# Moving the second layer norm's last step two slots earlier in a fused cross-attention layer, and writing its reciprocal root with one more VectorE instruction

## The reference

```python
q = (query @ Wq + bq); k = (key @ Wk + bk); v = (values @ Wv + bv)      # split into 16 heads
scores = einsum('bhqd,bhkd->bhqk', q, k) / sqrt(32)
scores = where(j < i, scores, -1e30); attn = softmax(scores)            # row 0 is set to 0
attn_out = einsum('bhqk,bhkd->bhqd', attn, v) @ Wo + bo
x = layer_norm(query + attn_out, ln1_g, ln1_b)
ffn = relu(x @ W1 + b1) @ W2 + b2
out = layer_norm(x + ffn, ln2_g, ln2_b)
# layer_norm(x) = (x - mean) * rsqrt(var + 1e-5) * g + b
```

## Time and profile before

| | |
|---|---|
| median of three runs | 2712.73 us |
| profiled execution, its own time | 2712.73 us |
| span from the first to the last instruction | 2710.8 us |
| TensorE busy (matmul) | 2620.6 us, 97% |
| VectorE busy | 2098.2 us, 77% |
| GpSimd busy | 1582.1 us, 58% |
| ScalarE busy | 1529.8 us, 56% |
| mean granted TensorE clock | 0.986 |

### The profile page before, as it was taken

One profiled execution on the slowest core, in us unless ns is written; L12 is line 12 of the kernel. 1 busy time (PEld: TensorE's weight loads), 2 busy tenths in 40 slices (PEclk: granted clock), 3 DMA queues, 4 the chain that ended last, 5 costly groups with the idle time before them and its releaser, 6 DMA issues.

```text
span 2710.8 us, 61812 instructions
## 1 busy us (share of the span) xinstructions
PE 2620.6 (97%) x22604; PEld 2241.0 (83%) x22604; DVE 2098.2 (77%) x4723; ACT 1529.8 (56%) x2945; POOL 1582.1 (58%) x1724
## 2 busy tenths in 40 slices
PE   7999999999999999977999999999999999999998
PEld 5888888888888888765888888888888888888887
DVE  6888888888888888877767766777767676767675
ACT  4777777777777777766434343444343444444443
POOL 3777777766666666655545454555545555555553
PEclk9999999999999999987999999999999999999999
DMA  6556555655555555555322231323232323132220
GB/s 191 149 147 157 144 147 146 159 148 142 149 135 134 138 138 133 141 134 142 98 53 69 50 70 49 70 49 72 54 69 50 71 49 70 49 69 52 67 54 26
DMA packets 439552, 273.31 MB, mean 101 GB/s; under 512 B 299648, under 2 KB 334400, under 8 KB 439248
## 3 DMA queue, kind: packets, MB, share of 16 engines
q1 hardware_dynamic: 438288, 267.79, 39.6%
q10 hardware_dynamic: 960, 1.57, 0.3%
HBM read 109.86 MB, written 57.67 MB: 62 GB/s over the span
## 4 chain that ended last, share of the span: by engine, by line
PE 83%; DVE 10%; issue 3%; DMA 1%; SPq 1%; POOL 1%; ACT 1%; ACTq 0%; DVEq 0%; POOLq 0%
PE h_ps L1359 24%; PE acc L1375 21%; PE lin_ps L707 10%; PE front L1345 6%; PE lin_ps L703 5%; PE max_ps L682 5%; PE st_ps L729 4%; PE o_ps L749 3%; PE o_ps L751 2%; DVE max_ps L660 2%; PE st_ps L764 2%; DVE xT L509 2%; DVE V L628 1%; DVE negmax_parts L603 1%; DVE W L1266 1%
## 5 line engine op out<-in xcount | busy, mean ns | idle before, releaser
L422 POOL TENSOR_TENSOR prob_lo<-probs,prob_hi 128x512 f16<-128x512 f32 (+1 forms) x768 | 788.1, 1041 | 408.7 <-ACT prob_hi L501 406.9
L1359 PE MATMUL h_ps<-x_halves,W 128*128 128x256 f16 x6144 | 756.5, 273 | 5.7 <-ACT hf L1173 5.7
L1359 PEld LDWEIGHTS h_ps<-x_halves,W 128*128 128x128 f16 x6144 | 596.5, 98 | 92.0 <-issue 15.9
L1375 PE MATMUL acc<-W,hs 128*128 128x256 f16 x5376 | 669.5, 273 | 1.1 <-DVE hs L1319 1.0
L1173 ACT ACTIVATE hf<-h_ps,b1s,scale_evac 128x256 f32<-128x256 f32 x512 | 284.4, 561 | 548.4 <-PE h_ps L1359 546.3
L1375 PEld LDWEIGHTS acc<-W,hs 128*128 128x128 f16 x5376 | 525.9, 98 | 62.4 <-issue 1.6
L499 ACT ACTIVATE probs<-st_ps 128x512 f32<-128x512 f32 (+1 forms) x768 | 406.9, 530 | 287.5 <-PE st_ps L764 248.6
L660 DVE CUSTOM_DVE_ANT_0 max_ps<-max_ps,mask_q 128x256 f32<-128x256 f32 (+2 forms) x768 | 421.7, 563 | 136.6 <-PE max_ps L682 136.3
L1099 POOL TENSOR_TENSOR hf<-hf 128x256 f32<-128x256 f32 x256 | 241.0, 941 | 471.4 <-ACT hf L1173 470.9
L501 ACT ACTIVATE prob_hi<-st_ps 128x512 f16<-128x512 f32 (+1 forms) x768 | 407.9, 531 | 0.0
L1319 DVE TENSOR_TENSOR hs<-hf,hs 128x896 f16<-128x896 f32 x256 | 285.8, 1136 | 154.1 <-ACT hs L1162 154.1
(11 more groups left out here) (120 smaller groups left out, 3845.3 us busy)
## 6 DMA issues: line engine op xcount, KB each, us to landing
heads<-stage SPq DMA_DIRECT2D x756, 128.0 KB, 2.4
raw<-in_xT SPq DMA_DIRECT2D x64, 256.0 KB, 3.1
o_in<-ctx_rows SPq DMA_DIRECT2D x256, 64.0 KB, 2.7
x_in<-in_x SPq DMA_DIRECT2D x32, 512.0 KB, 4.1
x_rows<-x SPq DMA_DIRECT2D x64, 256.0 KB, 2.0
o_in<-x_rows SPq DMA_DIRECT2D x256, 64.0 KB, 2.4
out<-y SPq DMA_DIRECT2D x32, 512.0 KB, 3.1
raw<-in_cT SPq DMA_DIRECT2D x60, 256.0 KB, 3.6
```

Source lines behind the costliest of these rows:

```text
L422: pool.tensor_tensor(prob_lo[:, k % 4, 0:w], probs[:, k % PROBS, 0:w], prob_hi[:, k % 4, 0:w], ALU.subtract).then_inc(pl_done, 1)
L1359: last = pe.matmul(h_ps[:, f % 2, 0:T], W1[:, aw, j, f * P:(f + 1) * P], x1_halves[:, item.parity, aa, j, :], start=(j == 0 and m == 0), s ...
L1375: last = pe.matmul(acc_products[:, n, :], hs[:, p % HS, aa, n, :], W2[:, p, aw, n, :], start=(p == 0 and m == 0 and n % 2 == 0), stop=(p = ...
```

## The change

`NORM2`, the slot of the second layer norm's root on ScalarE and of its `normalise` on VectorE, goes from `RES2 + 8` to `RES2 + 6`, that is from slot 14 of a window to slot 12; `STORE` goes from `RES2 + 9` to `RES2 + 8`, slot 15 to slot 14. In `normalise`, which both layer norms use, the Newton step z = r(1.5 - 0.5 r r ve) is written with four instructions behind the reciprocal in place of three.

```diff
-    NORM2 = RES2 + 8
-    STORE = RES2 + 9
+    NORM2 = RES2 + 6
+    STORE = RES2 + 8
...
-    LNS = 2 * U + 4
+    LNS = 2 * U + 5
...
             dve.reciprocal(r, sd[:, norm, :]).then_inc(ln_step[norm], 1)
             wait_for(dve, ln_step[norm], LNS, item, 2 * U + 2)
-            dve.scalar_tensor_tensor(out=t, in0=r, scalar=-0.5, in1=r, op0=ALU.mult, op1=ALU.mult
-                                     ).then_inc(ln_step[norm], 1)
+            dve.tensor_tensor(t, r, r, ALU.mult).then_inc(ln_step[norm], 1)
             wait_for(dve, ln_step[norm], LNS, item, 2 * U + 3)
             dve.tensor_tensor(t, t, ve[:, norm, :], ALU.mult).then_inc(ln_step[norm], 1)
             wait_for(dve, ln_step[norm], LNS, item, 2 * U + 4)
-            dve.scalar_tensor_tensor(out=z, in0=t, scalar=1.5, in1=r, op0=ALU.add, op1=ALU.mult
-                                     ).then_inc(ln_root[norm], 1)
+            dve.tensor_scalar(t, t, -0.5, 1.5, ALU.mult, ALU.add).then_inc(ln_step[norm], 1)
+            wait_for(dve, ln_step[norm], LNS, item, 2 * U + 5)
+            dve.tensor_tensor(z, r, t, ALU.mult).then_inc(ln_root[norm], 1)
```

## The result

The changed kernel takes 2759.2 us, the median of four runs (2754.3 to 2761.5), against 2712.2 for the kernel before (2711.5 to 2712.9). The ratio is 1.0171, with a 95% interval from 1.0153 to 1.0188: 1.7% slower, 47.0 us (41 to 51 by the interval), where 2760.3 us were forecast. The profiled execution took 2753.78 us, with a span of 2751.9.

The account below looks back on a forecast made before the run. TensorE, busy 1350.00 of 1350.00 us in the second stage, was taken as the bound. 30 windows x 1.57 = 47.1, plus 0.2 and 0.3, gave 47.6 us on 2712.73: 2760.3 us, range 2722 to 2778.

Parts of the forecast that it names:

- What bounds the kernel, and through what: Second stage: TensorE always busy, so the change can only lose; margin of 2.84 us at tile 15, through evacuation 13.
- The turns with GpSimd: Second norm's chain on VectorE: instructions wait for GpSimd's running ones, including b2 additions; TensorE loses 1.57 us per window.
- the working: One window's chain after the change: reciprocal 2014.57, transpose 2020.94, evacuation 13 to 2023.72, tile 15 at 2023.77 (was 2022.20).
- The tensor_scalar: New one-input VectorE step in `normalise`: waits in turn too, or else the sum is 0.2 us per window lower; left open.
- Thirty windows, and it does not wear off: Full windows: root and GpSimd's sums both hang on evacuation 11, so the stall returns; 30 x 1.57 = 47.1 us.
- A second stall: Next window's tile 0: just fits with 0.3 us to spare; as a rival, another 1 us per window, 2790 us, chance 0.07.
- The signs named: Profile after: TensorE short about 1.6 us per window; last small step 1.2, first large step 1.7, high half waits 5.
- The rival without a meeting with the additions: Second norm's chain misses the b2 additions; evacuation 13 is 0.27 us ahead of tile 15; 2713.2 us, chance 0.11.
- The other edits: Fourth small step outside the second norm's chain, hidden behind TensorE's full queue in 29 windows: 0.2 + 0.3 us.
- the 0.2 priced: Very end of the kernel, nothing beside the chain: the fourth small step adds 0.19 us.
- The 0.3 us put down for the first windows: First layer norm in the first three windows, where TensorE has gaps: the fourth small step costs perhaps 0.3 us in all.
- The store: Earlier `STORE`: block reads queued behind it need both transposes done, so no cost, no gain.

Follow-up runs that it names:

- slot 13: The changed kernel with NORM2 in slot 13 in place of 12 (`RES2 + 7`), STORE in slot 14: 2720.2 us, ratio 1.0033.
- slot 11: The changed kernel with NORM2 one slot earlier still (`RES2 + 5`), ScalarE's root behind evacuation 10 instead of 11: 2711.7 us, ratio 1.0000.

## Why the prediction was right

*What bounds the kernel, and through what.* Right: TensorE's queue was full, so the change could only lose, and it lost at tile 15 through evacuation 13, which stands on ScalarE behind a wait for VectorE's transpose.

*The turns with GpSimd.* Right in each step checked. From the start of evacuation 11, the working had the reciprocal 0.68 us on, the large steps at 3.74 and the transpose at 7.05; measured are 1985.70, 1988.75 and 1992.06 less 1985.01, that is 0.69, 3.74 and 7.05. Tile 15 stood at 9.88 in the working and stands at 9.85. That the two engines take turns was read from a handful of rows and now shows in 30 windows. The experiment with the additions of b2 two slots later shows that this, and not the amount of work ahead of the transpose, makes the loss.

*The tensor_scalar.* Left open between waiting and not; it waits. Asked for at 1987.11, it ends at 1987.50 with GpSimd's line 1102 (1987.47), where it takes 0.17 with GpSimd idle (2010.58 above). The trace of the kernel before could have settled it, with the `tensor_scalar` of `variance`, which takes 0.17 undisturbed (at 2003.35) and here ends with GpSimd's sum:

```profile
2010.30 0.73 POOL L1100 TENSOR_TENSOR hf<-hf 128x256 f32<-128x256 f32 x1
2010.57 0.48 DVE L1190 TENSOR_SCALAR ve<-mv 128x2 f32<-128x2 f32 x1
```

The reciprocal, with one input as well, does not wait: it takes 0.15 to 0.17 in all 64 places of either trace, also right behind the start of a sum (1985.70). The rule of the Trainium skill cited there ("SBUF — State Buffer", "SBUF: two separate sides") agrees.

*Thirty windows, and it does not wear off.* Right: 30 waits of 1.18 or 1.19, and 30 x 1.55 = 46.5 us. The experiment with the root behind evacuation 10 shows why: root and GpSimd's sums hang on the same evacuation. That the totals agree to 0.6 us (47.6 and 47.0) is luck all the same, as the interval reaches from 41 to 51. The two profiled executions differ by 41.1: 7.7 less ahead of the first evacuation of line 1173, 3.6 more in the first two windows (1.55 of it the first stall), 45.0 more in the 29 that follow, and 0.2 at the end.

*A second stall.* Right that it just fits. It was put at 0.3 us ahead of tile 0; the second low half ends at 1996.84 and tile 0 starts at 1997.16. With the chain in slot 13 this is the place where 0.2 us per window is lost.

*The signs named.* The last small step (1.18 for 1.2), the first large step (1.72 in 30 windows, for 1.7) and the high half's wait (4.92 for 5) came as said. TensorE's busy time does not fall short by 1.6 us per window but by 1.18; the rest of the 1.55 shows only in the distance of starts.

*The rival without a meeting with the additions.* It was priced too tight. The run with the additions later is that case, and its large steps start 2.72 us behind evacuation 11 (2014.91 to 2017.63), where the rival's sum has 2.92: it gives the fourth step 0.4 and not the 0.2 that it adds undisturbed. So 0.51 us are left ahead of tile 15, and not 0.27.

*The other edits.* Here the sum was right and the reason was not. At the very end, the chain takes 0.99 us from the reciprocal to the large steps (2746.25 to 2747.24), against 0.78 before (2705.43 to 2706.21), the 0.2 priced. Outside the second norm's chain, the fourth instruction was priced at 0.2 to 0.5 us in all, because TensorE's queue covers it. Put alone into the kernel before, in both norms, it costs 13 us. In the change the first norm's is covered all the same: the `hs` of slot 8 ends 1.87 us ahead of need in every full window, where it was 0.4 to 2.1. The likely reason is that the second norm's chain no longer stands ahead of the `hs` of slot 14 and the store is out of the way early; no run takes the two apart. So the sum held, but the reason given for this term ("hidden behind TensorE's full queue") says nothing of the margin, and by it I expected 2712.4 to 2713.0 us of the Newton step alone, which took 2724.3. The 0.3 us put down for the first windows is not borne out either: they took 2.0 us more than the stall, in this one pair of profiles, and the spread ahead of 1340 us is larger than that.

*The store.* No cost, as worked out: the block reads behind it start at 1995.14, as soon as the second transpose is over, though the store itself went out at 1991.16.

Two things stay open. Why VectorE's lateness differs from window to window before the change was not settled; in the later windows the reads ahead of the projection also take longer on the queue (5.8 to 6.9 us instead of 5.5 from the first block read to `x_in`), which fits, but no run took them apart, and in the change such reads (5.9 to 6.2) in the last windows leave the distance of 46.4 as it is. And the runs of one kernel spread by some 7 to 12 us, of which the profiles put a good part ahead of 1340 us: there the profiled execution of the change is 7.7 us ahead of that of before (first evacuation of line 1173 at 1247.69 and 1255.43), without any edit in that stretch that would make it faster.

## What to carry to other kernels

When an instruction moves, ask which instruction of another engine is started by the same event; two engines released together meet in every round, and a move of one slot may end it (slot 11: nothing lost) or leave a small rest (slot 13: 9.7 us). Read a full queue not as cover but as a margin: note, in the latest round, how far ahead of need each result comes, before an extra instruction is called free. A VectorE instruction that lasts several times its usual length, with the end of a GpSimd instruction at its own end, is waiting, though the profile counts it as busy. Measure a loss by the distance of equal instructions, window by window: a delay of 0.2 us in each window appears in no list of waits.

## What was not expected of the hardware

The exactness of the turns. In the change, 30 instructions of 128x2 took about 1.18 us each behind an addition of 128x512, for 0.16 undisturbed, and being 0.02 to 0.16 us later than GpSimd's request decides it. (Within some hundredths the starts shown do not tell the order: in the earlier trace rows a request shown 0.02 ahead waited too.) And a loss is not in proportion to the work added: 0.2 us more per chain cost 13 us in a kernel in which TensorE had never waited from 1340 us on, and two of them together with an earlier slot cost nothing (2711.7 us).
